# Turning shift rows and chunk results with transposing DMAs instead of TensorE, and spreading the last pair's shortcut over six turns

## The chip, the cores and the metric

The kernel runs on one core of a Trainium2 chip. The engines of the core work from instruction queues of their own and wait for each other through semaphores: TensorE (PE: matmuls, and PEld: the loading of their stationary operand), VectorE (DVE), ScalarE (ACT), GpSimd (POOL), and SyncE (SP), which here only issues DMAs. SBUF is the on-chip memory, PSUM holds what PE writes. The metric is the device time of one execution in microseconds, the median of several runs.

## The reference

Group normalisation of x, then eight heads of attention over the 2304 pixels of each image with 1x1 convolutions as projections, a shortcut convolution, and a residual:

```python
x: (4, 512, 48, 48) f32;  Wq, Wk, Wv, Wsc: (512, 512);  gamma: (1, 512, 1, 1)
xn = groupnorm(x, 32 groups)
q, k, v = Wq xn, Wk xn, Wv xn            # 8 heads of 64
attn = softmax(q^T k)                    # 2304 x 2304 for each image and head
out  = attn v                            # back to channels x pixels
result = x + gamma * out + Wsc xn
```

## The kernel before, in words

**Tiling.** The work is cut into 16 blocks (4 images x 4 pairs of heads, numbered g), and each block into 6 chunks of 384 query pixels (c = 0 to 5, `n` = 6g + c, 96 in all). A chunk runs over the 2304 keys in 18 steps of 128 keys, two steps to a **turn** (`m` = 0 to 8). Every f32 product is made of fp16 or bf16 parts, so that each of its matmuls has a partner for the lower half.

**One turn** issues on PE, in this order (from line 477): `top(U)` (scores for the row maxima of the chunk that comes 22 steps later), two `score` (L416 and L421: the scores of this chunk, the shift added by a matmul with the row CR in steps 0 and 1 of a chunk), `top(U + 1)`, two `weigh` (L439 to L442: the weighted sum of v for the two steps of the turn before, into the PSUM bank OB), and then half of a projection for the next block (`project`, 12 or 36 matmuls in sixths; L349 and L352). In turns 1 and 2 the projection is the shortcut of this chunk (`sc`); in turns 3 to 8 it is a part of k, q or v of the next block, in the order of `AHEAD`: chunks c = 0, 1, 2 make two k parts each (ready in turns 4 and 6), the others v and q. In the last pair (g = 15) turns 3 to 8 have no projection.

**The other engines.** ACT makes the exponentials (`exps`, L542) into PE32, of which four buffers exist, copies half of the maxima's scores to MXC, copies projections out of PSUM (`leave`), and evacuates OB into Oe in turn 0 of the next chunk (L556). DVE makes the maxima (L690, L693, L698), the lower halves of q and v, and the additions into xr: the shortcut (L672), and the attention's result (L680). POOL makes the lower half of each exponential (`split`, L895, two a turn), the differences of keys (`keys_diff`, L876, and `keys_diff_lower`, L882: for a k part two and three turns after it is ready, so in turns 6 and 7, and 8 and 0), and in some chunks the lower halves of the next image's normalised pieces (L970, turns 5 to 8 of chunks 3 to 5 in six of the blocks). A `weigh` waits for its `split`, a `split` for its exponential, and each queue is in order.

**The shift.** In turn 7 DVE reduces the maxima of the next chunk to c16, [128, 3, 128] fp16 with queries on the partitions (`shift_parts`, L703, L708, L710). In turn 8 PE turns it by three matmuls with an identity into free columns of the score banks (`shift_rows`, L368), ACT copies it to CR as fp16 (L535), and PE's first `score` of the next chunk waits for CR (line 406).

**The result of a chunk.** Oe has queries on the partitions and the sum of weights beside the sums. DVE inverts the sums in turn 1 of the next chunk (L717), POOL divides in turn 2 (L889; in the last pair ACT does, L565), PE turns the quotient, f32, in turn 0 of the chunk after that by three transposes into PJ (`turn`, L377), and DVE adds gamma times it into xr in turn 1 (L680), which SP then stores. SP's queue per chunk: the piece of x for the statistics or the normalisation, the store of chunk n-2, the load of chunk n+1's x into xr.

Of the kernel before, what the change touches and what calls it, by code (L numbers as in the profile page):

```python
# [35 lines left out]
CHUNKS = BLOCKS * NCH  # L36
DS = MT // 2
# [16 lines left out]
def slot_unit(n, m):  # L54

    if m == 0:
        return None
    if m < 3:
        return ("sc", n)
    g, c = divmod(n, NCH)  # L60
    if g + 1 == BLOCKS:
        return None
    kind, part = AHEAD[3 * c + (m - 3) // 2]
    return (kind, g + 1, part)


def done_at(M):

    if M < 0 or M % DS == 0 or M % DS % 2 == 1:
        return None  # L70
    return slot_unit(M // DS, M % DS)

# [9 lines left out]
def units():  # L82

    out = [(kind, 0, c) for kind, c in FIRST + BESIDE]
    for n in range(CHUNKS):
        if n >= 2:
            out.append(("f", n - 2))
        out += [done_at(n * DS + m) for m in range(DS) if done_at(n * DS + m)]
    out += [("f", CHUNKS - 2), ("f", CHUNKS - 1)]
# [13 lines left out]
LAST = (BLOCKS - 1) * NCH  # L103


def build(nc, x, wq, wk, wv, wsc, gamma, out):
    ctx = ExitStack()
    with ctx:
# [15 lines left out]
        attn = sb("attn", [P, 2, CH], F32)  # L124
# [3 lines left out]
        CR = sb("CR", [P, CH], F16)  # L128
# [43 lines left out]
        def shift_bank(n):  # L172
            if n == 0:
                return OB[:, 0:CH].rearrange("p (i n) -> p i n", i=QT)
            return SLS[:, 0:QT, CH:CH + P]

# [29 lines left out]
        s_wt = sem("s_wt")  # L206
        s_y = sem("s_y")
# [14 lines left out]
        s_cp = sem("s_cp")  # L222
# [35 lines left out]
        def _(sp):  # L258
# [14 lines left out]

            rows = x[0:C, :].rearrange("(t p) n -> p t n", p=P)
# [9 lines left out]
            for n in range(CHUNKS):  # L284
# [16 lines left out]
                if n + 1 < CHUNKS:  # L301
                    load_x(n + 1)
            store(CHUNKS - 2)
# [5 lines left out]
        def _(pe):  # L309
# [53 lines left out]
            def shift_rows(n):  # L363
                if n:
                    pe.wait_ge(s_exp, n * MT)
                pe.wait_ge(s_cc, 3 * n + 3)
                for i in range(QT):
                    last = pe.matmul(shift_bank(n)[:, i, :], c16[:, i, :], identh[:, :], start=True, stop=True)  # L368
                last.then_inc(s_cp, 1)

            def turn(n):
# [4 lines left out]
                for i in range(QT):  # L376
                    last = pe.transpose(PJ[:, i * P:(i + 1) * P], attn[:, n % 2, i * P:(i + 1) * P], identf[:, :])  # L377
# [19 lines left out]
            def score(n, k):  # L397
# [7 lines left out]
                if k == 0:  # L405
                    pe.wait_ge(s_cr, n + 1)
# [6 lines left out]
                if k < 2:  # L413
                    for h in range(2):
                        r = slice(h * D, (h + 1) * D)
                        pe.matmul(SL[k % 2][:, h, 0:CH], ones[r, :], CR[r, :], start=True, stop=False,  # L416
# [52 lines left out]
            for i, (kind, c) in enumerate(BESIDE):  # L469
                if i == len(BESIDE) - 1:  # L470
                    shift_rows(0)
# [5 lines left out]
            for n in range(CHUNKS):  # L477
                for m in range(DS):
# [18 lines left out]
                    if root_unit(n, m):  # L497
                        root(*root_unit(n, m)[1:])
                    if u and m % 2 == 0:
                        project(u, 4, 6)  # L500
            weigh(STEPS - 2)
            weigh(STEPS - 1)
            turn(CHUNKS - 2)
# [3 lines left out]
        def _(act):  # L507
# [25 lines left out]
            def shift_rows(n):  # L533
                act.wait_ge(s_cp, n + 1)
# [24 lines left out]
            def divide(n):  # L559

                act.wait_ge(s_rc, n + 1)
                act.wait_ge(s_pj, PLACE["f", n - 2] + 1)
                for h in range(2):
                    for i in range(QT):
                        one = act.activation(attn[:, n % 2, i * P + h * D:i * P + (h + 1) * D], Oe[:, h, i, 0:D],  # L565
                                             ACT.Copy, scale=rc[:, h, i, :])
# [433 lines left out]
```

## Time and profile before

| | us |
|---|---|
| median of 3 runs | 3211.22 (3210.1 to 3211.5) |
| the profiled execution | 3213.72 |
| its span, first to last instruction | 3212.0, at a mean granted TensorE clock of 0.999 |
| busy: PE / POOL / DVE / ACT | 3146.4 / 2811.2 / 2115.8 / 2095.1 |
| chain that ended last: PE / POOL / issue / ACT | 67% / 24% / 4% / 2% |
| DMA: mean rate, share of 16 engines (q1) | 26 GB/s, 7.4% |

Busy time is the time in which an engine worked on an instruction; matmuls overlap, so a busy PE is not one at its peak. The chain is followed back from the last instruction to what released each. A row of a timeline has the start in us, the duration in us, the engine, the line of the kernel, the operation and its tiles (out<-in), the count of instructions merged into it, and in brackets the idle time of the engine before it with what ended it. A row without a bracket began with no wait seen.

### The profile page before, as it was taken

Reading aid. Unit: us, or ns where it says so; the run is one execution under the profiler, and the core shown is the slowest. Engines: PE = TensorE matmul, PEld = TensorE weight load, DVE = VectorE, ACT = ScalarE, POOL = GpSimd, SP = SyncE. Lnnn points to the kernel's source line nnn. Section 1 sums busy time; section 2 is a strip of 40 time slices with the busy share of each in tenths; the row PEclk is TensorE's granted clock in tenths of the full one; section 3 lists DMA queues with packets and bytes.
Section 4 is the critical chain, followed back from the end, with each engine's and each line's share of the span. In section 5 each row is a group of like instructions: output and inputs, shape, how many; then the busy total and the mean of one; then the engine's idle time right before and its main releaser. Section 6 shows DMA issues by size and latency. Waiting matters only on the chain.

```text
span 3212.0 us, 119957 instructions
## 1 busy us (share of the span) xinstructions
PE 3146.4 (98%) x52880; PEld 2151.1 (67%) x52880; DVE 2115.8 (66%) x3539; ACT 2095.1 (65%) x3473; POOL 2811.2 (88%) x2128
## 2 busy tenths in 40 slices
PE   5999999999999999999999999999999999999998
PEld 3666676666667666676666766667666666766665
DVE  7767666666677666666667666666666666666674
ACT  3566676676666677676666567767666666666675
POOL 2688999999898899999989889999988989888898
PEclk9999999999999999999999999999999999999999
DMA  3010010100011001010001101001000000000000
GB/s 126 24 37 22 25 33 14 36 22 17 22 37 42 17 22 37 22 34 15 12 27 42 37 12 37 22 27 32 17 12 15 15 12 17 12 17 12 17 17 14
DMA packets 53030, 82.66 MB, mean 26 GB/s; under 512 B 4384, under 2 KB 50464, under 8 KB 52512
## 3 DMA queue, kind: packets, MB, share of 16 engines
q1 hardware_dynamic: 52512, 74.99, 7.4%
q8 instruction: 418, 6.85, 0.9%
q14 instruction: 100, 0.82, 0.1%
HBM read 56.10 MB, written 18.87 MB: 23 GB/s over the span
## 4 chain that ended last, share of the span: by engine, by line
PE 67%; POOL 24%; issue 4%; ACT 2%; DVE 0%; POOLq 0%; DVEq 0%
POOL PLO L895 19%; PE SL L421 17%; PE PJ L352 13%; PE OB L439 9%; PE MX L393 8%; PE OB L442 7%; PE OB L441 7%; PE PJ L349 4%; POOL DF L876 3%; POOL QK L882 2%; ACT PE L542 1%; PE PJ L377 1%; PE SL L416 1%; ACT QK L523 0%; PE SL L368 0%
## 5 line engine op out<-in xcount | busy, mean ns | idle before, releaser
L895 POOL TENSOR_TENSOR PLO<-PE 128x768 f16<-128x768 f32 x1728 | 2498.8, 1472 | 334.3 <-ACT PE L542 325.8
L542 ACT ACTIVATE PE<-SL 128x768 f32<-128x768 f32 x1728 | 1310.7, 815 | 14.7 <-PE SL L421 14.6
L439 PEld LDWEIGHTS OB<-V,PE 128*128 128x128 bf16 x10368 | 949.3, 99 | 278.7 <-POOL PLO L895 151.5
L690 DVE TENSOR_REDUCE mx<-MX 128x1 f32<-128x384 f32 x864 | 481.0, 557 | 969.6 <-PE MX L393 969.6
L439 PE MATMUL OB<-V,PE 128*128 128x65 f16 x10368 | 1069.6, 194 | 17.6 <-POOL PLO L895 16.8
L441 PE MATMUL OB<-V,PE 128*128 128x64 f16 x10368 | 1060.0, 193 | 0.0
L442 PE MATMUL OB<-V,PLO 128*128 128x65 f16 x10368 | 1059.0, 196 | 0.0
L550 ACT ACTIVATE MXC<-MX 128x384 f32<-128x384 f32 x864 | 424.6, 491 | 915.2 <-PE MX L393 901.6
L421 PE MATMUL SL<-QK 64*128 64x384 f16 x10368 | 999.4, 323 | 0.0
L441 PEld LDWEIGHTS OB<-V,PE 128*128 128x128 bf16 x10368 | 966.3, 97 | 0.0
L442 PEld LDWEIGHTS OB<-V,PLO 128*128 128x128 f16 x10368 | 965.8, 98 | 0.0
L693 DVE TENSOR_REDUCE mx<-MX 128x2 f32<-128x768 f32 x864 | 822.8, 952 | 29.9 <-PE MX L393 3.5
L421 PEld LDWEIGHTS SL<-QK 64*128 64x128 f16 x10368 | 505.5, 94 | 285.4 <-issue 0.8
L352 PE MATMUL PJ<-X,WT 128*128 128x384 f16 x3324 | 639.7, 326 | 0.0
L393 PE MATMUL MX<-QK 64*128 64x384 f16 x3456 | 572.4, 328 | 5.9 <-ACT MXC L550 2.9
L698 DVE TENSOR_REDUCE mx<-MXC 128x1 f32<-128x384 f32 x864 | 476.8, 552 | 4.2 <-ACT MXC L550 3.9
L352 PEld LDWEIGHTS PJ<-X,WT 128*128 128x128 f16 x3324 | 286.5, 98 | 136.3 <-issue 0.3
L393 PEld LDWEIGHTS MX<-QK 64*128 64x128 f16 x3456 | 182.0, 93 | 288.0 <-issue 180.7
L349 PE MATMUL PJ<-WT,X 128*128 128x128 f16 x3240 | 214.9, 219 | 0.0
L349 PEld LDWEIGHTS PJ<-WT,X 128*128 128x128 f16 x3240 | 186.0, 98 | 0.0
L882 POOL TENSOR_TENSOR QK<-DF,QK 128x384 f16<-128x384 f32 x96 | 89.2, 930 | 16.5 <-ACT QK L511 16.5
L535 ACT ACTIVATE CR<-SL 128x384 f16<-128x384 f32 x95 | 46.7, 491 | 84.5 <-PE SL L368 84.5
(108 smaller groups left out, 1435.8 us busy)
## 6 DMA issues: line engine op xcount, KB each, us to landing
gx<-x SPq DMA_DIRECT2D x36, 768.0 KB, 4.5
xr<-x SPq DMA_DIRECT2D x96, 192.0 KB, 2.4
out<-xr SPq DMA_DIRECT2D x96, 192.0 KB, 1.9
X<-x SPq DMA_DIRECT2D x6, 768.0 KB, 8.9
QK<-wk SPq DMA_DIRECT2D x1, 1024.0 KB, 12.7
QK<-wq SPq DMA_DIRECT2D x1, 1024.0 KB, 13.4
QK<-wv SPq DMA_DIRECT2D x1, 1024.0 KB, 14.1
QK<-wsc SPq DMA_DIRECT2D x1, 1024.0 KB, 15.3
```

What stands on the lines that cost most here:

```text
L349: last = pe.matmul(dst[:, i * P:(i + 1) * P], X[:, b % 2, p, t, m * P:(m + 1) * P], WT[:, 2, wp, t, j * P:(j + 1) * P], **edge)
L352: last = pe.matmul(dst[:, 0:CH], WT[:, WEIGHT[kind], wp, t, j * P:(j + 1) * P], X[:, b % 2, p, t, c * CH:(c + 1) * CH], **edge)
L393: last = pe.matmul(MX[:, h, 0:CH], QK[r, g % 2, QH, c * CH + i * P:c * CH + (i + 1) * P], QK[r, g % 2, KH, t * CH:(t + 1) * CH], start=Tru ...
L421: last = pe.matmul(SL[k % 2][:, h, 0:CH], QK[r, g % 2, a, keys], QK[r, g % 2, b, q], start=False, stop=a == DH and b == QL, skip_group_che ...
L439: pe.matmul(acc, upper, v[:, D:V1], start=k == 0 and h == 0 and i == 0, stop=False, skip_group_check=True)
L441: pe.matmul(acc[:, 0:D], upper, v[:, 0:D], start=False, stop=False, skip_group_check=True)
L442: last = pe.matmul(acc, PLO[:, s % PB, p0:p0 + P], v[:, D:V1], start=False, stop=k == MT - 1 and h == 1 and i == QT - 1, skip_group_check= ...
L542: act.activation(PE32[:, s % PB, :].rearrange("p (h n) -> p h n", h=2), SL[s % 2][:, :, 0:CH], ACT.Exp, scale=1.0 / SS).then_inc(s_exp, 1)
L690: nc.vector.tensor_reduce(mx3[:, n % 2, 0, k:k + 1], MX[:, 0, 0:CH], AX.X, ALU.max).then_inc(s_mxf, 1)
L693: nc.vector.tensor_reduce(mx3[:, n % 2, :, k], MX[:, :, 0:CH], AX.X, ALU.max).then_inc(s_mxf, 1)
L698: nc.vector.tensor_reduce(mx3[:, n % 2, 1, k:k + 1], MXC[:, :], AX.X, ALU.max).then_inc(s_mxr, 1)
L895: nc.gpsimd.tensor_tensor(PLO[:, s % PB, :], PE32[:, s % PB, :], PE32[:, s % PB, :].bitcast(BF16)[:, 1:4 * CH:2], ALU.subtract).then_inc(s ...
```

## The change

- The shift: PE's three matmuls, their columns in the score banks and ACT's copy go. SP issues one transposing DMA from c16 to CR, which becomes [128, 3, 128] of the same 384 columns. The first `score` waits for it. In SP's queue it stands after the load of chunk n+1's x; the one for chunk 0 right ahead of that for chunk 1.
- The result of a chunk: ACT divides, for all chunks, in turns 2 and 4 (three 64-column pieces of one head each), and writes an fp16 copy of the quotient in turn 6 (`result_upper`); POOL writes the rest as fp16 in turn 7 (`result_lower`), ahead of that turn's key difference and splits; SP turns both halves by one transposing DMA of 768 columns (`results`), behind the shift rows' DMA; DVE adds gamma times each into xr in turns 2 and 4 of the chunk after the one in which it is divided (`add_result`). `turn` on PE stays for the last chunk alone. attn has one buffer instead of two.
- The last pair: the shortcut is made one sixth a turn in turns 1 to 6, instead of half in each of turns 1 and 2.
- In the two chunks of an image where PE makes a small matmul for the next statistics in turn 8 (`root`), it still stands before the last third of the projection.

The core of the diff:

```diff
@@ planning
+    if n >= LAST:
+        return ("sc", n) if m < 7 else None
     if m < 3:
         return ("sc", n)
...
+def sixths(n, m):
+
+    if n >= LAST:
+        return m - 1, m
+    return (0, 3) if m % 2 else (3, 6)
@@ SyncE
+            def shift_rows(n):
+
+                sp.wait_ge(s_cc, 3 * n + 3)
+                sp.dma_start_transpose(CR[:, :, :], c16[:, :, :].rearrange("p i n -> p (i n)")).then_inc(s_cr, 16)
+
+            def results(n):
+
+                sp.wait_ge(s_al, n + 1)
+                sp.wait_ge(s_fo, n)
+                sp.dma_start_transpose(back[:, :, :], half[:, :, :].rearrange("p l n -> p (l n)")).then_inc(s_at, 16)
...
                 if n + 1 < CHUNKS:
                     load_x(n + 1)
+                if n == 0:
+                    shift_rows(0)
+                if n + 1 < CHUNKS:
+                    shift_rows(n + 1)
+                if n:
+                    results(n - 1)
@@ TensorE
-            def shift_rows(n):
-                if n:
-                    pe.wait_ge(s_exp, n * MT)
-                pe.wait_ge(s_cc, 3 * n + 3)
-                for i in range(QT):
-                    last = pe.matmul(shift_bank(n)[:, i, :], c16[:, i, :], identh[:, :], start=True, stop=True)
-                last.then_inc(s_cp, 1)
...
-                    pe.wait_ge(s_cr, n + 1)
+                    pe.wait_ge(s_cr, 16 * (n + 1))
...
-                    if m == 0 and n >= 2:
-                        turn(n - 2)
                     u = slot_unit(n, m)
-                    if u:
-                        project(u, *((0, 3) if m % 2 else (3, 4)))
-                    if m == DS - 1 and n + 1 < CHUNKS:
-                        shift_rows(n + 1)
@@ ScalarE
-                act.activation(CR[:, :].rearrange("p (i n) -> p i n", i=QT), shift_bank(n), ACT.Copy
-                               ).then_inc(s_cr, 1)
...
+            def divide(n, h):
+
+                if h == 0:
+                    act.wait_ge(s_rc, n + 1)
+                    act.wait_ge(s_al, n)
+                for i in range(QT):
+                    one = act.activation(attn[:, i * P + h * D:i * P + (h + 1) * D], Oe[:, h, i, 0:D],
+                                         ACT.Copy, scale=rc[:, h, i, :])
+                if h == 1:
+                    one.then_inc(s_wt, 1)
+
+            def result_upper(n):
+                act.wait_ge(s_wt, n + 1)
+                if n:
+                    act.wait_ge(s_at, 16 * n)
+                act.activation(half[:, 0, :], attn[:, :], ACT.Copy).then_inc(s_ah, 1)
...
-                    if m == 2 and n > LAST:
-                        divide(n - 1)
+                    if n and m in (2, 4):
+                        divide(n - 1, m // 2 - 1)
+                    if n and m == 6:
+                        result_upper(n - 1)
@@ VectorE
+            def add_result(n, l):
+
+                j = n // NCH % PAIRS
+                if l == 0:
+                    dve.wait_ge(s_pjd, LEFT["sc", n])
+                    dve.wait_ge(s_at, 16 * (n + 1))
+                else:
+                    dve.wait_ge(s_fh, n + 1)
+                nc.vector.scalar_tensor_tensor(
+                    out=xr[:, n % 3, :], in0=back[:, l * QT:(l + 1) * QT, :].rearrange("p i n -> p (i n)"),
+                    scalar=gam[:, j:j + 1], in1=xr[:, n % 3, :],
+                    op0=ALU.mult, op1=ALU.add).then_inc(s_fo if l else s_fh, 1)
...
-                    if m == 1 and n >= 2:
-                        leave(("f", n - 2))
...
+                    if m in (2, 4) and n >= 2:
+                        add_result(n - 2, m // 2 - 1)
@@ GpSimd
-                nc.gpsimd.tensor_tensor(
-                    attn[:, n % 2, :].rearrange("p (i h d) -> p h i d", h=2, d=D), Oe[:, :, :, 0:D],
-                    rc[:, :, :, :].to_broadcast([P, 2, QT, D]), ALU.mult).then_inc(s_wt, 1)
+            def result_lower(n):
+                pool.wait_ge(s_ah, n + 1)
+                nc.gpsimd.tensor_tensor(half[:, 1, :], attn[:, :], half[:, 0, :], ALU.subtract).then_inc(s_al, 1)
...
-                    if m == 2 and 0 < n <= LAST:
-                        divide(n - 1)
+                    if m == 7 and n:
+                        result_lower(n - 1)
```

## Rows read from the trace of the kernel before

**Rows 1.** Page, part 1: busy us, share of the span, instructions of each engine.

```profile
PE 3146.4 (98%) x52880; PEld 2151.1 (67%) x52880; DVE 2115.8 (66%) x3539; ACT 2095.1 (65%) x3473; POOL 2811.2 (88%) x2128
```

**Rows 2.** Timeline of ACT, evacuations into chunks 43 and 44: start us, us.

```profile
1505.58 0.50 ACT L556 ACTIVATE Oe<-OB 128x390 f32<-128x390 f32 x1 [0.40 <-PE OB L442]
...
1538.45 0.50 ACT L556 ACTIVATE Oe<-OB 128x390 f32<-128x390 f32 x1 [0.39 <-PE OB L442]
```

**Rows 3.** Timeline of PE, end of chunk 43 and start of 44.

```profile
1534.46 0.33 PE L368 MATMUL SL<-identh,c 128*128 128x128 f16 x3
1534.63 0.83 PE L349 MATMUL PJ<-WT,X 128*128 128x128 f16 x12
...
1535.57 0.33 PE L416 MATMUL SL<-CR,ones 64*128 64x384 f16 x2
...
1538.25 0.52 PE L377 MATMUL PJ<-identf,attn 128*128 128x128 f32 x3
1538.70 0.34 PE L393 MATMUL MX<-QK 64*128 64x384 f16 x2
...
1540.11 0.20 PE L439 MATMUL OB<-V,PE 128*128 128x65 f16 x1
...
1541.09 0.20 PE L439 MATMUL OB<-V,PE 128*128 128x65 f16 x1 [0.25 <-POOL PLO L895]
```

**Rows 4.** Timeline of POOL, turn 5 of chunk 43 to 0 of 44.

```profile
1523.06 2.89 POOL L895 TENSOR_TENSOR PLO<-PE 128x768 f16<-128x768 f32 x2 [1.36 <-ACT PE L542]
...
1537.25 0.93 POOL L882 TENSOR_TENSOR QK<-DF,QK 128x384 f16<-128x384 f32 x1
1538.12 4.33 POOL L895 TENSOR_TENSOR PLO<-PE 128x768 f16<-128x768 f32 x3
```

**Rows 5.** Timeline of DVE, turn 7 of chunk 43.

```profile
1530.66 1.45 DVE L710 SCALAR_TENSOR_TENSOR c<-cmx,c 128x6 f16<-128x6 f32 x1
```

**Rows 6.** Timeline, end of plain chunk 46 and start of 47.

```profile
1629.22 0.41 DVE L710 SCALAR_TENSOR_TENSOR c<-cmx,c 128x6 f16<-128x6 f32 x1
...
1633.63 0.33 PE L416 MATMUL SL<-CR,ones 64*128 64x384 f16 x2
...
1635.49 5.93 POOL L895 TENSOR_TENSOR PLO<-PE 128x768 f16<-128x768 f32 x4 [1.15 <-ACT PE L542]
...
1638.74 0.19 PE L439 MATMUL OB<-V,PE 128*128 128x65 f16 x1
```

**Rows 7.** Timeline of POOL, start of chunk 42, behind normalised pieces.

```profile
1472.12 5.92 POOL L895 TENSOR_TENSOR PLO<-PE 128x768 f16<-128x768 f32 x4 [0.45 <-ACT PE L542]
```

**Rows 8.** Groups of instructions by line: busy us, mean ns of one | idle before.

```profile
L882 POOL TENSOR_TENSOR QK<-DF,QK 128x384 f16<-128x384 f32 x96 | 89.2, 930 | 16.5 <-ACT QK L511 16.5
...
L680 DVE SCALAR_TENSOR_TENSOR xr<-PJ,gam,xr 128x384 f32<-128x384 f32 x96 | 58.4, 608 | 9.8 <-PE PJ L377 9.8
```

**Rows 9.** One line each, L710 and L267: duration ns min/median/max, first and last start us.

```profile
L710 DVE SCALAR_TENSOR_TENSOR c<-cmx,c x96: 186/778/1470, 91.3 to 3170.4; 128x6 f16<-128x6 f32 x96
...
L267 SPq DMA_DIRECT2D xr<-x x96: 327/328/1215, 20.2 to 3156.8; - x96
```

**Rows 10.** Page, part 6: DMA issues, KB each, median us from issue to landing.

```profile
gx<-x SPq DMA_DIRECT2D x36, 768.0 KB, 4.5
xr<-x SPq DMA_DIRECT2D x96, 192.0 KB, 2.4
out<-xr SPq DMA_DIRECT2D x96, 192.0 KB, 1.9
```

**Rows 11.** Timelines of POOL, PE and ACT, a chunk of the last pair.

```profile
3095.81 0.50 ACT L556 ACTIVATE Oe<-OB 128x390 f32<-128x390 f32 x1 [0.52 <-PE OB L442]
...
3123.78 0.50 ACT L556 ACTIVATE Oe<-OB 128x390 f32<-128x390 f32 x1 [0.52 <-PE OB L442]
...
3105.01 17.15 POOL L895 TENSOR_TENSOR PLO<-PE 128x768 f16<-128x768 f32 x12 [0.70 <-ACT PE L542]
...
3120.89 0.34 PE L416 MATMUL SL<-CR,ones 64*128 64x384 f16 x2 [0.36 <-issue]
```

More of the change, by code:

```diff
@@ L36 @@
 CHUNKS = BLOCKS * NCH
+LAST = (BLOCKS - 1) * NCH
 DS = MT // 2
@@ L60, in slot_unit @@
     g, c = divmod(n, NCH)
-    if g + 1 == BLOCKS:
-        return None
     kind, part = AHEAD[3 * c + (m - 3) // 2]
     return (kind, g + 1, part)
+def sixths(n, m):
+    if n >= LAST:
+        return m - 1, m
+    return (0, 3) if m % 2 else (3, 6)
 def done_at(M):
-    if M < 0 or M % DS == 0 or M % DS % 2 == 1:
+    if M < 0:
         return None
-    return slot_unit(M // DS, M % DS)
+    n, m = divmod(M, DS)
+    u = slot_unit(n, m)
+    return u if u and sixths(n, m)[1] == 6 else None
 def root_unit(n, m):
@@ L85, in units @@
     for n in range(CHUNKS):
-        if n >= 2:
-            out.append(("f", n - 2))
         out += [done_at(n * DS + m) for m in range(DS) if done_at(n * DS + m)]
-    out += [("f", CHUNKS - 2), ("f", CHUNKS - 1)]
+    out.append(("f", CHUNKS - 1))
     return out
@@ L123, in build @@
         xr = sb("xr", [P, 3, CH], F32)
-        attn = sb("attn", [P, 2, CH], F32)
+        attn = sb("attn", [P, CH], F32)
+        half = sb("half", [P, 2, CH], F16)
+        back = sb("back", [P, 2 * QT, P], F16)
         Oe = sb("Oe", [P, 2, QT, AW], F32)
@@ L206, in build @@
         s_wt = sem("s_wt")
+        s_ah = sem("s_ah")
+        s_al = sem("s_al")
+        s_at = sem("s_at")
+        s_fh = sem("s_fh")
         s_y = sem("s_y")
@@ L376, in turn @@
                 for i in range(QT):
-                    last = pe.transpose(PJ[:, i * P:(i + 1) * P], attn[:, n % 2, i * P:(i + 1) * P], identf[:, :])
+                    last = pe.transpose(PJ[:, i * P:(i + 1) * P], attn[:, i * P:(i + 1) * P], identf[:, :])
                 last.then_inc(s_pj, 1)
@@ L415, in score @@
                         r = slice(h * D, (h + 1) * D)
-                        pe.matmul(SL[k % 2][:, h, 0:CH], ones[r, :], CR[r, :], start=True, stop=False,
+                        pe.matmul(SL[k % 2][:, h, 0:CH], ones[r, :], CR[r, :, :], start=True, stop=False,
                                   skip_group_check=True)
@@ L489, in _ @@
                         weigh(s - 1)
-                    if m == 0 and n >= 2:
-                        turn(n - 2)
                     u = slot_unit(n, m)
-                    if u:
-                        project(u, *((0, 3) if m % 2 else (3, 4)))
-                    if m == DS - 1 and n + 1 < CHUNKS:
-                        shift_rows(n + 1)
-                    if root_unit(n, m):
+                    lo, hi = sixths(n, m)
+                    if u and root_unit(n, m):
+                        project(u, lo, hi - 2)
                         root(*root_unit(n, m)[1:])
-                    if u and m % 2 == 0:
-                        project(u, 4, 6)
+                        project(u, hi - 2, hi)
+                    elif u:
+                        project(u, lo, hi)
             weigh(STEPS - 2)
             weigh(STEPS - 1)
-            turn(CHUNKS - 2)
             turn(CHUNKS - 1)
@@ L557, in evacuate @@
                     "p (h i x) -> p h i x", h=2, x=OW)[:, :, :, 0:AW], ACT.Copy).then_inc(s_oe, 1)
[L559 to L566, printed above, removed]
-                one.then_inc(s_wt, 1)
+            def divide(n, h):
[12 more added lines that the diff above has]
+                act.activation(half[:, 0, :], attn[:, :], ACT.Copy).then_inc(s_ah, 1)
             def weights(w):
@@ L603, in _ @@
                     keys_diff_upper(("k", 0, i))
-            shift_rows(0)
             leave((BESIDE[-1][0], 0, BESIDE[-1][1]))
@@ L680, in leave @@
                     nc.vector.scalar_tensor_tensor(
-                        out=xr[:, n % 3, :], in0=src, scalar=gam[:, j:j + 1], in1=xr[:, n % 3, :],
+                        out=xr[:, n % 3, :], in0=src, scalar=gam[:, PAIRS - 1:PAIRS], in1=xr[:, n % 3, :],
                         op0=ALU.mult, op1=ALU.add).then_inc(s_fo, 1)
-                    dve.wait_ge(s_fo, n + 1)
-                    dve.sem_inc(s_pjd, 1)
+            def add_result(n, l):
[9 more added lines that the diff above has]
+                    op0=ALU.mult, op1=ALU.add).then_inc(s_fo if l else s_fh, 1)
             def top(U):
```

26 lines of the change are left out of this document (5 added, 21 removed).

## The prediction

> **What bounds the kernel now.** I read the page's busy shares first [rows 1]: PE is busy 98% of the span, POOL 88%, DVE and ACT two thirds. So PE is the bound on average, with POOL close behind. An average hides where in a chunk each of them is last, so next I read the timelines of PE and POOL across a chunk's end. One chunk takes 32.87 us, from one evacuation of the weighted sums to the next [rows 2], in nine turns of about 3.6 us.
>
> On PE [rows 3] the reader is to see three places. In turn 8 the three matmuls that turn the shift rows hold PE from 1534.46 to 1534.63, 0.17 us. In turn 0 the fp32 transposes hold it from 1538.25 to 1538.70, 0.45 us. In turn 1 the second `weigh` starts at 1541.09 behind a wait for POOL; the first one started at 1540.11, and its six steps of 0.093 us would have put the second at 1540.67, so PE loses 0.42 us there.
>
> On POOL [rows 4] the reader is to see where idle time (a bracket) stands. POOL waits 1.36 us for the exponentials of turn 5 and from 1523.06 on has no bracket until the last `split` of turn 0 ends at 1538.12 + 2 x 1.43 = 1540.98; PE starts 0.11 later. These 17.9 us are five pairs of splits (2.86 each), two lower halves of key differences (0.88 each, 1537.25 to 1538.12) and, with the remaining 1.9, the two differences themselves. So at this boundary POOL, not PE, is last. Key differences exist only in chunks whose number in the pair (c) is 0, 1 or 2, so this holds at the ends of those: 45 boundaries ahead of the last pair. After c = 3, 4, 5 POOL has rest: it waits 1.15 us before turn 0's splits in a plain chunk [rows 6], and 0.45 in the 18 chunks that also make normalised pieces [rows 7].
>
> **The change part by part.** *Off PE.* Each boundary loses 0.17 + 0.45 = 0.62 us of PE time [rows 3]; over 90 boundaries that would be 56 us, if PE were last at all of them.
>
> *POOL.* The division leaves turn 2, and the subtraction for the lower half comes into turn 7. It has the form of L882 (128x384, f32 minus f16 into f16): 930 ns busy [rows 8], 0.88 start to start [rows 4]. The place decides: turn 2 lies ahead of POOL's rest, turn 7 behind it. At the 45 boundaries after c = 0, 1, 2 the chain from turn 5's exponentials to turn 1's `weigh` has no rest to take it in, so it ends 0.88 later and none of PE's 0.62 is seen: PE waits longer. Freeing turn 2 returns nothing, since POOL waits ahead of turn 5's splits either way. That is 45 x 0.88 = +39.6.
>
> At the 27 plain boundaries after c = 3, 4, 5 the rest of 1.15 takes in the 0.88. POOL starts turn 0's splits at 1635.49 and ends the second at 1638.35, usable at 1638.46, and PE's second `weigh` starts at 1638.74 [rows 6]: a slack of 0.28. After the change turn 0 starts 0.17 earlier, the splits are usable at 1638.29, and PE is there at 1638.74 - 0.62 = 1638.12: it waits 0.17. Gain 0.45 each, 27 x 0.45 = -12.2. At the 18 with pieces the rest is 0.45 [rows 7]: the splits move 0.88 - 0.45 = 0.43 later, 0.28 of it is slack, and each is 0.15 slower: +2.7.
>
> *ACT.* It loses the CR copy and gets three 64-column divisions in each of turns 2 and 4 and a 384-column copy in turn 6. ACT is busy 65% [rows 1] and does these behind the exponentials of their turn, while it waits for PE: nothing. Without that cover, up to 0.3 us a turn.
>
> *DVE.* The last addition (turn 1, out of PSUM) becomes two, in turns 2 and 4, with both inputs in SBUF. L710 is such an instruction: six columns, 186 ns at least and 1470 at most [rows 9], which is the length of a split. So it waits for the POOL instruction under way, and I take it that POOL then waits for it. The Trainium skill ("SBUF — State Buffer", "Who interferes with whom") says that a two-input DVE instruction and a GpSimd instruction that reads SBUF hold a shared port in turn; the trace agrees. A 384-column one takes 0.61 by L680 [rows 8], with 1.43 of waiting 2.0 in the worst case; DVE is idle 34% of the span [rows 1], 1.2 us a turn. I cost it at nothing, since the wait is full only where a split has just begun, and at the upper end at 0.3 us in each of two turns, 180 x 0.3 = 54. POOL is held 0.4 us twice a chunk, ahead of its rest: nothing, except in the last pair.
>
> *SP and the transposing DMAs.* SP issues `shift_rows` once c16 is ready, behind `store` and `load_x`, which are done by turn 5, and ahead of `results`, which waits for POOL's lower half. Behind a late `shift_rows` only `results` is queued; for CR PE waits, with everything behind it. PE needs CR at turn 0's first score, 1535.57 [rows 3]; c16 was ready at 1530.66 + 1.45 = 1532.11 [rows 5]. That leaves 3.46 - 0.17 = 3.29 us; at a plain end 1633.63 - 1629.63 - 0.17 = 3.83 [rows 6]. No transposing DMA is in the trace. The nearest rows are a store of 192 KB at 1.9 us to landing and a load of 192 KB at 2.4; the far bound is the 768 KB piece at 4.5 [rows 10]. With the 0.33 that the issue takes [rows 9] these are 2.2, 2.7 and 4.8. An earlier landing than 2.2 gains nothing. CR is 96 KB, so I take 2.7: hidden. `results` has more than a turn and a half and is hidden at 4.8 too. The Trainium skill gives two answers: "Advanced Engine Details and Errata", "X-Bar Transpose (TRN2)", has such transfers as fast as regular ones, which agrees with my choice; by "VectorE: DVE Perf Modes", "The three transpose paths", one 128x128 block takes 1309 ns, an estimate of 4.2 for three in a row with the issue, and some 3255 us in all. No run here shows which.
>
> *The last pair.* A chunk takes 27.97 us [rows 11], with turns 1 and 2 long on PE, so that POOL waits there, and twelve splits on POOL without rest after them; it rests 2.1 in all. Spreading the shortcut removes the rests, and POOL's 25.9 + 0.88 + 2 x 0.4 (DVE) = 27.5 becomes the chunk. Four whole chunks gain 0.4, the last, without maxima, loses about 0.9: -1. The tail loses one turn and one DVE addition (0.45 and 0.61): -1.1. PE's wait for CR there, 0.36 now [rows 11], lies inside POOL's time.
>
> **The sum.** +39.6 - 12.2 + 2.7 - 1 - 1.1 = +28. The profiled execution took 3213.7 (span 3212.0 and 1.7 around it), so 3241.7; the median of the runs is 2.5 below it, so 3239.
>
> **The rivals.** *POOL isn't moved (faster).* Place: POOL in turns 5 to 8 after c = 0, 1, 2. If the lower half is taken in there, these boundaries stay as they are, since POOL is last at them already, and those with pieces gain 0.45 like the plain ones: -12.2 - 8.1 - 2.1 = -22, so 3189. The sum turns negative once POOL's chain ends less than 12/45 = 0.26 us later. For it: POOL's spans are rough in a profile, and short waits may hide in them. Against it: no bracket in 17.9 us. Only if POOL were last nowhere would all of PE's 56 us come, 3154. *The DMA lands late.* At 4.8 us it is 1.5 late after c = 0, 1, 2, where POOL's backlog hides it (turn 0's splits start at 1539.0 after the change; the exponentials would be there at about 1538.8), but 0.97 late at plain ends: 27 x 0.97 = 26, some 10 at the ones with pieces, some 8 in the last pair: +44, 3283. It begins to count from 3.8 us, and past 4.8 every microsecond costs about 95. The skill's 1309 ns would lie between. *It does not do what it says.* Spreading the shortcut may move nothing, as POOL sets the last pair: 2 us, inside the range.
>
> **How the numbers follow.** POOL last and the DMA hidden or nearly so: 0.55, 3239, own range 3220 to 3262 (the added 0.88 between 0.6 and 1.0, and some DVE delay). DMA late up to 4.8, or DVE's port waits nearly in full: 0.18, up to 3295. DMA later still: 0.10. POOL not moved: 0.14, 3189. All of PE's gain: 0.03. The range 3186 to 3295 holds the first, second and fourth; it leaves out the other two and a little of the edges. 0.2% of the time, 6.4 us, is about what a measurement can tell from no change: faster 0.15, within it 0.07 (the ways between 3189 and the forecast), slower 0.78.
>
> **What would show it.** In the profile after: POOL without a bracket from turn 5 to turn 1 after c = 0, 1, 2; PE's waits in turns 0 and 1 there grown from 0.42 to about 1.9 us together, chunks of 33.7 us there and 0.45 shorter than now at plain ends; L416 without idle time ahead of it; the transposes landing within 3.3 us of their release; DVE's additions of 0.5 to 2 us. The prediction is wrong if PE waits at L416 (DMA) or at L393 for DVE (ports), or if the chunks after c = 0, 1, 2 take 32.9 or less.

## The result and the profile after

The changed kernel takes 3242.8 us (median of 4 runs, 3241.8 to 3244.3) against 3211.4 for the kernel before in the same comparison: the ratio is 1.0098, with a 95% interval of 1.0086 to 1.011. The profiled execution took 3244.25, its span is 3242.4, and the granted clock was 0.998 (0.999 before). The forecast was 3239.

From the page of the kernel after: the busy shares; the chain that ended last, by engine; two groups (busy us, mean ns | idle before, releaser); and the two transposing DMAs (count, median us to landing).

```profile
PE 3112.3 (96%) x52307; PEld 2114.0 (65%) x52307; DVE 2245.6 (69%) x3634; ACT 2194.2 (68%) x4012; POOL 2882.4 (89%) x2133
...
PE 56%; POOL 33%; issue 4%; ACT 3%; DVE 1%; POOLq 0%; ACTq 0%; DVEq 0%
...
L913 POOL TENSOR_TENSOR PLO<-PE 128x768 f16<-128x768 f32 x1728 | 2552.5, 1502 | 293.9 <-ACT PE L547 290.2
...
L702 DVE SCALAR_TENSOR_TENSOR xr<-back,gam,xr 128x384 f32<-128x384 f16 x190 | 226.8, 1194 | 5.4 <-DMA back<-half 5.3
...
CR<-c SPq DMA_TRANSPOSE x96, 2.3
back<-half SPq DMA_TRANSPOSE x95, 2.8
```

PE's busy time is 34 us below [rows 1], and the kernel is 31 us slower: the work left PE, and its share of the last chain went to POOL, 33% where it was 24%. The waits say whom PE waits for (us, times, longest):

```profile
PEld OB L455 <- POOL PLO L913: 223.4, 569, 1.1
PE OB L455 <- POOL PLO L913: 72.1, 116, 1.0
ACT QK L521 <- POOL DF L898: 65.9, 46, 1.5
```

PE's matmuls of `weigh` waited 16.8 us for splits in the kernel before, and now 72.1. The third line is new in size (14.4 before): ACT's upper halves of key differences wait for the differences on POOL.

POOL's timeline at the end of a chunk with key differences, which answers to [rows 4]:

```profile
1539.09 2.89 POOL L913 TENSOR_TENSOR PLO<-PE 128x768 f16<-128x768 f32 x2 [1.05 <-ACT PE L547]
1541.94 1.00 POOL L898 TENSOR_TENSOR DF<-KF 128x384 f32<-128x384 f32 x1
1542.90 2.89 POOL L913 TENSOR_TENSOR PLO<-PE 128x768 f16<-128x768 f32 x2
1545.75 0.92 POOL L909 TENSOR_TENSOR half<-attn,half 128x384 f16<-128x384 f32 x1
1546.63 0.91 POOL L904 TENSOR_TENSOR QK<-DF,QK 128x384 f16<-128x384 f32 x1
1547.50 2.89 POOL L913 TENSOR_TENSOR PLO<-PE 128x768 f16<-128x768 f32 x2
1550.35 1.00 POOL L898 TENSOR_TENSOR DF<-KF 128x384 f32<-128x384 f32 x1
1551.31 2.89 POOL L913 TENSOR_TENSOR PLO<-PE 128x768 f16<-128x768 f32 x2
1554.16 0.92 POOL L904 TENSOR_TENSOR QK<-DF,QK 128x384 f16<-128x384 f32 x1
1555.04 5.74 POOL L913 TENSOR_TENSOR PLO<-PE 128x768 f16<-128x768 f32 x4
```

The reader is to see that no row after 1539.09 has a bracket, up to the end of turn 1's splits, and that L909 at 1545.75 stands in that row: 0.88 us from its start to the next one's. It is the lower half of the results, which the change put there. PE at the same place, which answers to [rows 3]:

```profile
1549.02 0.20 PE L455 MATMUL OB<-V,PE 128*128 128x65 f16 x1
...
1550.44 0.21 PE L455 MATMUL OB<-V,PE 128*128 128x65 f16 x1 [0.70 <-POOL PLO L913]
...
1552.29 0.33 PE L432 MATMUL SL<-CR,ones 64*128 64x384 f16 x2
...
1556.65 0.19 PE L455 MATMUL OB<-V,PE 128*128 128x65 f16 x1
...
1557.98 0.20 PE L455 MATMUL OB<-V,PE 128*128 128x65 f16 x1 [0.62 <-POOL PLO L913]
```

By the brackets PE waits for POOL 0.70 us in turn 8 and 0.62 in turn 1, where it waited 0.25 in turn 1 alone. Counted from start to start, as the prediction had its 0.42, these are 0.86 and 0.77: the first `weigh` starts at 1549.02 and at 1556.65, and 0.56 later the second was due. The score of turn 0, which needs the turned shift rows, starts without idle time. On DVE and SP's queue, when the shift rows were ready and when their DMA was issued:

```profile
1546.69 0.89 DVE L731 SCALAR_TENSOR_TENSOR c<-cmx,c 128x6 f16<-128x6 f32 x1
...
1547.61 1.19 SPq L284 DMA_TRANSPOSE CR<-c  x1
```

c16 is ready at 1547.58, the median of such DMAs lands 2.3 us after its issue, and PE wants the rows 4.7 us after c16. ACT's evacuations of the weighted sums, at the ends of this chunk and of a plain one, answer to [rows 2]:

```profile
1521.44 0.50 ACT L561 ACTIVATE Oe<-OB 128x390 f32<-128x390 f32 x1 [0.40 <-PE OB L458]
1555.17 0.50 ACT L561 ACTIVATE Oe<-OB 128x390 f32<-128x390 f32 x1 [0.40 <-PE OB L458]
...
1621.72 0.50 ACT L561 ACTIVATE Oe<-OB 128x390 f32<-128x390 f32 x1 [0.40 <-PE OB L458]
1653.65 0.50 ACT L561 ACTIVATE Oe<-OB 128x390 f32<-128x390 f32 x1 [0.40 <-PE OB L458]
```

33.73 us the one, 31.93 the other. All such distances of both traces, by the number c of the chunk in its pair, typical value in us; the last column sums the differences of the 89 chunks ahead of the last pair:

| c | before | after | sum |
|---|---|---|---|
| 0 | 32.45 | 32.86 | +5.7 |
| 1 | 32.88 | 33.75 | +13.0 |
| 2 | 32.86 | 33.73 | +12.3 |
| 3, plain / with pieces | 32.84 / 32.84 | 32.84 / 33.48 | +3.9 |
| 4, plain / with pieces | 32.37 / 32.38 | 31.92 / 32.57 | -3.0 |
| 5, plain / with pieces | 32.26 / 32.26 | 31.80 / 32.53 | -2.5 |

Together +29.5. The chunks c = 2 of blocks 1, 5 and 9, which have the square-root unit (`root`), are in the sums only: they take 34.84 for 34.19. With the start (-0.4), the last pair's first chunk (-0.7) and its other five (+2.2), and the tail (-0.2) that is the span's +30.4, but for rounding.

### The profile page after: what moved, and what is told of

The parts are those of the page before. It is cut to its first block, busy times and chain, and to the rows that moved or that the text cites. A ratio compares the mean times of both kernels' runs of the same rounds, so it can differ in the third digit from the quotient of the medians.

```text
span 3242.4 us, 119546 instructions
## 1 busy us (share of the span) xinstructions
PE 3112.3 (96%) x52307; PEld 2114.0 (65%) x52307; DVE 2245.6 (69%) x3634; ACT 2194.2 (68%) x4012; POOL 2882.4 (89%) x2133
## 4 chain that ended last, share of the span: by engine, by line
PE 56%; POOL 33%; issue 4%; ACT 3%; DVE 1%; POOLq 0%; ACTq 0%; DVEq 0%
POOL PLO L913 25%; PE SL L437 15%; PE PJ L376 12%; PE OB L455 8%; PE MX L409 7%; PE OB L458 6%; PE OB L457 6%; PE PJ L373 3%; POOL DF L898 3%; POOL QK L904 2%; ACT PE L547 2%; POOL half L909 2%; POOL X L988 1%; PE SL L432 1%; ACT QK L533 1%
## 5 line engine op out<-in xcount | busy, mean ns | idle before, releaser
L913 POOL TENSOR_TENSOR PLO<-PE 128x768 f16<-128x768 f32 x1728 | 2552.5, 1502 | 293.9 <-ACT PE L547 290.2
L455 PE MATMUL OB<-V,PE 128*128 128x65 f16 x10368 | 1074.8, 194 | 79.1 <-POOL PLO L913 72.1
L555 ACT ACTIVATE MXC<-MX 128x384 f32<-128x384 f32 x864 | 423.3, 490 | 874.8 <-PE MX L409 874.8
L702 DVE SCALAR_TENSOR_TENSOR xr<-back,gam,xr 128x384 f32<-128x384 f16 x190 | 226.8, 1194 | 5.4 <-DMA back<-half 5.3
L570 ACT ACTIVATE attn<-Oe,rc 128x64 f32<-128x64 f32 x570 | 155.6, 345 | 0.0
```

The source lines that it names most:

```text
L455: pe.matmul(acc, upper, v[:, D:V1], start=k == 0 and h == 0 and i == 0, stop=False, skip_group_check=True)
L913: nc.gpsimd.tensor_tensor(PLO[:, s % PB, :], PE32[:, s % PB, :], PE32[:, s % PB, :].bitcast(BF16)[:, 1:4 * CH:2], ALU.subtract).then_inc(s ...
```

## The experiments

My theory: POOL's extra 0.88 us in turn 7, where it is last, takes 0.88 at 45 ends, and PE's gain is seen only at the others. The rivals: DVE's additions hold POOL through the shared port; the DMA for the shift rows lands too late; the key differences hold the ends anyway, wherever the lower half stands. Chunk lengths below are distances of evacuations as in the table.

**The lower half two turns earlier.** `lower_turn5` (the comments behind # stand only here):

```
-                    if n and m == 6:     # ACT: result_upper
+                    if n and m == 4:
-                    if m == 7 and n:     # POOL: result_lower
+                    if m == 5 and n:
```

> The changed kernel with the fp16 copy on ScalarE in turn 4 and POOL's lower half in turn 5, ahead of the wait of 1.05 us that POOL has there, instead of in turn 7. Theory (place on POOL's chain): the 0.88 us come off the 45 boundaries after c = 0, 1, 2 (-39.6) and about 0.6 off the 18 with normalised pieces (-11), so about 3192 us, chunks of 32.9 us after c = 0, 1, 2. Rival (DVE's two-input additions hold up POOL, whose splits grew from 1472 to 1502 ns on average, 52 us of busy time in all, and that is the added time): nothing moves, 3240 to 3245 us.

It took 3209.0 us (10 runs, 3206.0 to 3212.7; ratio to before 0.9991, 0.9982 to 1.0). So one subtraction, with the copy on ACT that it waits for, moved by two turns and nothing removed, is worth 34 us: the place decides. POOL's split stays at 1502 ns on average with the same DVE additions, so the port isn't what made the change slow. But it missed 3192 by 17. The larger part is the 18 chunks with pieces, where I expected -11: undisturbed they take 33.46, 32.56 and 32.52, as in the kernel after. POOL's timeline in one of them shows why:

```profile
1226.08 3.20 POOL L913 TENSOR_TENSOR PLO<-PE 128x768 f16<-128x768 f32 x2 [0.73 <-ACT PE L547]
1229.25 0.91 POOL L909 TENSOR_TENSOR half<-attn,half 128x384 f16<-128x384 f32 x1
1230.12 0.92 POOL L988 TENSOR_TENSOR X<-gx,X 128x384 f16<-128x384 f32 x1
...
1242.17 8.64 POOL L913 TENSOR_TENSOR PLO<-PE 128x768 f16<-128x768 f32 x6
```

No row from 1226.08 to 1242.17 has a further bracket. With pieces POOL's last rest is the one ahead of turn 4's splits, so turn 5 (L909) is still behind it, and the subtraction stays on the chain; an earlier turn wasn't tried. The remaining shortfall lies at the other ends: chunks with c = 1 or 2 were 32.87 where undisturbed, yet many were 0.8 to 1.2 longer. The trace has the reason for these: the group of matmuls that needs the shift rows (busy us, mean ns | idle before), and one instance:

```profile
L432 PE MATMUL SL<-CR,ones 64*128 64x384 f16 x384 | 63.2, 323 | 15.6 <-issue 15.6
...
585.60 1.19 SPq L284 DMA_TRANSPOSE CR<-c  x1
...
589.64 0.34 PE L432 MATMUL SL<-CR,ones 64*128 64x384 f16 x2 [0.65 <-issue]
```

Without POOL's delay PE is back at this score 3.4 us after the issue (589.64 - 0.65 - 585.60), and this transfer landed after 3.9. Such landings are the tail that the prediction did not have; the DMA view of 585.4 to 588 shows what else moved:

```profile
q1 hardware_dynamic: 414, 0.10, 18.5%
q8 instruction: 1, 0.02, 2.2%
...
CR<-c SPq DMA_TRANSPOSE x1, 3.9
```

A packet of instruction fetch (q8) came in between; from its share in this view it took about 0.9 us of one of the 16 DMA engines (an estimate, 2.2% of 16 x 2.6 us). I read this view for each of the 95 later issues of three traces. All 49 landings above 3.5 us had such a packet between issue and landing (6 in the kernel after, 19 here, 24 in `three_moves` below), and 14 of the 224 landings up to 2.5 us. That ties them together; which delays which, and how, wasn't tried. Nor do the late ones fall by chance: `lower_turn5` and `both_moves` have their slow landings at the same 20 of the 95 issues (one is 3.53 us here), and five of the six of the kernel after are at the same issues in `halves_last`.

**The second key difference later.** Applied to the kernel before, `before_keys_later`, and with the move above to the one after, `both_moves`:

```
-                    done = done_at(n * DS + m - 2)
-                    if done and done[0] == "k":
-                        keys_diff_upper(done)
+                    for late in (2, 4):
+                        done = done_at(n * DS + m - late)
+                        if done and done[0] == "k" and late == 2 + 2 * (done[2] % 2):
+                            keys_diff_upper(done)
...
-                    for late, do in ((2, keys_diff), (3, keys_diff_lower)):
+                    for late, do in ((2, keys_diff), (3, keys_diff_lower), (4, keys_diff), (6, keys_diff_lower)):
...
-                        if done and done[0] == "k":
+                        if done and done[0] == "k" and (late >= 4) == (done[2] % 2 == 1):
```

> The kernel before with one thing moved: of each chunk's second key part (c = 0, 1, 2) the difference on POOL and its fp16 copy on ScalarE go from turn 8 to turn 1 of the next chunk, the lower half from turn 0 to turn 3. Theory: POOL's chain from turn 5 to turn 1 loses 0.96 + 0.88 us and PE is last there; the wait of 0.42 us at 45 boundaries goes, -19 us, about 3192 us. Rival (PE alone sets the time, the wait of 0.42 is hidden by later slack): 3211 us. Second rival (POOL becomes late in turns 2 and 3, where it also divides): 3200 to 3225 us.

3201.3 us (6 runs, 3199.6 to 3203.2; ratio 0.9968, 0.9957 to 0.998). Of the kernel before, PE's 0.42 at the ends was POOL's too: 24 of the 30 chunks with c = 1 or 2 and all 15 with c = 3 are 0.35 to 0.41 shorter, some -14.4 in all. The other six, in blocks 1, 5 and 9 with the square-root unit, are longer (33.44 for 32.87 at c = 1, 35.01 for 34.19 at c = 2), +4.2, which the expectation didn't have. That and 14.4 for 19 make most of the 9 us by which it missed 3192.

> The changed kernel with both moves: POOL's lower half in turn 5, and the second key part's POOL work in turns 1 and 3 of the next chunk. Theory: POOL is then nowhere last ahead of the last pair, and PE's 0.62 us at 90 boundaries and the 0.42 at 45 come through, less about 0.17 at each boundary where the splits of turn 0 are just late for PE: 3211 - 56 - 19 + 16 = 3152 us. Rival (port holds or the transposing DMAs take the gain): above 3200 us.

3193.5 us (4 runs, 3191.5 to 3194.3; ratio 0.9943, 0.9928 to 0.9958). Faster than before, and 41 short of what I expected. The idle time at L432 is again 34.1 us over 42 waits of matmuls and loads, some 17 for PE; the 18 chunks with pieces stay at 32.5 to 32.8 where 31.9 was wanted, some 12; the last five chunks are 2.6 longer than before; the rest I didn't take apart. With POOL freed, the DMA is the next that comes late.

**And the shift a turn earlier.** `three_moves` is `both_moves` with DVE's shift rows made in turn 6:

```
-                    if m == 7 and n + 1 < CHUNKS:    # shift_parts
+                    if m == 6 and n + 1 < CHUNKS:
```

> The changed kernel with POOL's lower half in turn 5, the second key part's POOL work in turns 1 and 3 of the next chunk, and the reduction to c16 at the end of DVE's turn 6 instead of 7, which is when its last maximum is there, so that CR's DMA has a turn more. With the first two alone PE waited for CR at about 20 boundaries, some 17 us in all, where the landing took 3.8 to 4.5 us instead of 2.3. Theory: this wait goes, and 3 us in the last pair: about 3173 us. Rival (the wait for CR isn't the landing of the DMA, or something else takes its place): 3190 us or more.

3181.9 us (4 runs, 3181.9 to 3183.9; ratio 0.9906, 0.9892 to 0.9921). It is faster than both kernels. SP's queue and PE at one end, and the source views of L432 (idle before it: us, times) and of L284:

```profile
1453.57 1.19 SPq L284 DMA_TRANSPOSE CR<-c  x1
...
1460.52 0.33 PE L432 MATMUL SL<-CR,ones 64*128 64x384 f16 x2
...
  issue: 0.2, 1
...
DMA to landing us min/median/max: 2.3/2.3/5.0
```

PE now wants the rows 6.9 us after the issue, and the same tail, up to 5.0 us and 27 of 95 above 2.5, costs 0.2 us in all. This shows that the waits of `both_moves` were these landings. Of the nine that were missed against the expectation 3.9 lie at c = 3, 4, 5 of the three blocks with statistics (0, 4 and 8), 0.43 a chunk longer; I put that down to DVE's fuller turn 6, which wasn't tried.

**The margin alone.** `shift_turn6` has only that last edit on the kernel after:

> The changed kernel with only the reduction to c16 at the end of DVE's turn 6 instead of 7, so that CR's DMA starts a turn earlier. Theory (POOL's backlog hides CR's late landings everywhere ahead of the last pair): only the last pair gets what PE waited for CR there, about 3 us: 3239 us. Rival (late landings are a part of the added time ahead of the last pair): 3225 us, since about 20 of them by some 0.8 us were seen once POOL's backlog was gone.

3241.8 us (4 runs, 3240.7 to 3242.0; ratio 1.0092, 1.0077 to 1.0107), not to be told from after. Ahead of the last pair it gains nothing, since POOL's backlog hides what lands late, and it loses 0.43 in nine chunks (+3.9). The last pair's five chunks are 4.2 shorter (136.11 for 140.33). So that is what late landings cost the kernel after.

**The lower half twice.** `lower_twice` adds POOL's subtraction once more behind the first, into a spare tile:

```
+                nc.gpsimd.tensor_tensor(spare[:, :], attn[:, :], half[:, 0, :], ALU.subtract)
```

> The changed kernel with the lower half's subtraction made twice in turn 7 (the first into a spare tile that nothing reads). Theory: another 0.88 us at the 45 boundaries after c = 0, 1, 2 and at the 18 with pieces, about 0.6 at the 27 plain ones, whose rest of 1.15 is mostly used up, and 0.88 in the five last: +76 us, about 3319 us. Rival (POOL has room, being busy 89%; ports or DMAs are the cause): under 3255 us.

3305.5 us (4 runs, 3304.1 to 3307.8; ratio 1.0295, 1.0278 to 1.0312). Chunks with c = 1 or 2 are 34.62, the second 0.87 exactly as the first, and so are those with pieces. The plain ones took only 0.15 more (31.95 for 31.80), where I had given them 0.6: most of it still fell into POOL's rest. That is 27 x 0.45 = 12 of the 14 us between the expectation and the time.

**The DMA later.** `one_more_turned` and `two_more_turned` issue one or two further transposing DMAs of c16, into spare tiles, ahead of the real one:

```
+                sp.dma_start_transpose(spare0[:, :, :], c16[:, :, :].rearrange("p i n -> p (i n)")).then_inc(s_sp0, 16)
```

> The changed kernel with one more transposing DMA of c16, into a spare tile that nothing reads, ahead of each one into CR in SP's queue. SP takes 1.19 us to issue one, so CR lands some 1.3 us later at all 95 boundaries, 3.6 us after c16 is ready. Theory (the DMA is hidden, with room left before turn 0's first score: 3.8 us at plain ends, 4.7 after c = 0, 1, 2, 2.4 in the last pair): only the last pair's five boundaries pay, +6, and a few whose landing is late already, +4: about 3253 us. Rival (the landing of CR is on the path): +1.3 x 95, 3360 us.

3267.1 us (4 runs, 3263.0 to 3269.1; ratio 1.0169, 1.0153 to 1.0184): +24, and 14 above what I expected. The undisturbed chunks keep their lengths (33.76, 31.80), so the median landing, now 3.6 us after c16, is still in time; what is longer are single chunks in which the landing was late, by 0.6 to 2 us, and the last five chunks (144.7).

> The same with two more transposing DMAs ahead of the one into CR: CR lands about 4.9 us after c16 is ready, which is the case of the prediction's late DMA at 4.8. Theory: hidden behind POOL's backlog after c = 0, 1, 2, 1.1 us late at 27 plain ends (+30), about 0.6 at 18 with pieces (+11), 2.4 in the last pair (+12), and +10 where it is late already: about 3306 us; by the prediction's own price of the late case +44 on 3243, 3287 us. Rival (each boundary pays the whole lateness): 3242 + 95 x 1.1 or more, over 3340 us.

3325.5 us (4 runs, 3322.3 to 3327.5; ratio 1.035, 1.0333 to 1.0367): +83, and 19 above what I expected. SP's queue and PE at a plain end:

```profile
1645.88 1.19 SPq L288 DMA_TRANSPOSE spare<-c  x1
1647.11 1.25 SPq L289 DMA_TRANSPOSE spare<-c  x1
1648.40 1.26 SPq L290 DMA_TRANSPOSE CR<-c  x1
...
1650.91 0.34 PE L440 MATMUL SL<-CR,ones 64*128 64x384 f16 x2 [1.05 <-issue]
```

Each issue holds SP's queue 1.2 us, the real one lands 4.9 us after c16 was ready, and PE waits 1.05. Plain chunks are 1.17 longer (32.97), 27 x 1.17 = 32 of the 83. The rest is mostly the tail, which now hits at any end. As rival, the late DMA had the right mechanism; its price for 4.8 us, +44 in all, was too low, since it took every landing to be the median.

**The additions with one input.** `one_input_adds`:

```
-                nc.vector.scalar_tensor_tensor(
-                    out=xr[:, n % 3, :], in0=back[:, l * QT:(l + 1) * QT, :].rearrange("p i n -> p (i n)"),
-                    scalar=gam[:, j:j + 1], in1=xr[:, n % 3, :],
-                    op0=ALU.mult, op1=ALU.add).then_inc(s_fo if l else s_fh, 1)
+                nc.vector.tensor_scalar(
+                    xr[:, n % 3, :], back[:, l * QT:(l + 1) * QT, :].rearrange("p i n -> p (i n)"),
+                    gam[:, j:j + 1], None, ALU.mult).then_inc(s_fo if l else s_fh, 1)
```

> The changed kernel with DVE's two additions of the turned halves replaced by two multiplications by gamma that read only the turned half from SBUF; the shortcut and x are left out of the output by this. Theory: DVE no longer waits for POOL (1.24 us become under 0.6) nor holds it (POOL's splits back from 1502 to about 1472 ns on average), but POOL took those holds out of its rest, so only the last pair gets faster, by 0.64 us a chunk: about 3240 us. Rival (port holds are the added time): 3190 to 3200 us.

3239.9 us (4 runs, 3238.6 to 3240.8; ratio 1.0085, 1.007 to 1.01), 2.8 below after, as much as the last five chunks lose (137.41 for 140.33). My 0.64 us for each of these isn't there: undisturbed ones are 0.23 shorter (26.94 for 27.17), and the largest part is one late landing that was less late (28.67 for 30.59). The groups of both instructions in this kernel:

```profile
L702 DVE TENSOR_SCALAR xr<-back,gam x190: 413/1045/2514, 173.1 to 3232.6; 128x384 f32<-128x384 f16 x190
...
L912 POOL TENSOR_TENSOR PLO<-PE 128x768 f16<-128x768 f32 x1728 | 2517.7, 1483 | 325.8 <-ACT PE L547 321.9
```

POOL's splits are 35 us less busy (1483 ns each for 1502), and next to nothing of it reaches the end of the program; only chunks with pieces are some 0.14 shorter (32.43 for 32.57 at c = 4). The test is weaker than meant: the multiplication, 413 ns at least, still took 1045 in the median, so it was held up too.

**Each part alone.** `shift_only` has the shift rows by DMA and the results as before, `results_only` the other way round:

> The kernel before with only the shift rows turned by the transposing DMA; results, division and the last pair's shortcut as before. Theory: PE's 0.17 us come through at the 45 ends of c = 3, 4, 5 (-7.6) and not where POOL is last; about 20 of 95 landings take 3.8 us or more, and a part of these is seen, since there is no added backlog on POOL to hide them (+5 to +8): 3208 to 3213 us, no change that can be measured. Rival (the DMA is hidden and PE is the bound everywhere): -0.17 x 95, 3196 us.

3206.8 us (10 runs, 3205.8 to 3209.0; ratio 0.9985, 0.9976 to 0.9994). It gains 0.17 at the ends where PE is last (c = 0, 4 and 5: 32.28, 32.20, 32.09) and 2.2 in the last five chunks; at c = 1 and 2 the ends stay at 32.87 or become longer by a late landing. I had expected no change that could be measured.

> The changed kernel with the shift rows turned by PE and copied by ScalarE as before. Theory: the cost lies in the results' part: +0.88 us at 45 ends, +0.15 at 18, -0.28 at 27 (PE's transposes of 0.45 gone, of which 0.17 turns into waiting), +2 in the last pair, -1 at the end: 3212 + 36 = 3248 us. Rival (the shift's DMA is the cost): about 3200 us.

3249.4 us (4 runs, 3249.0 to 3250.9; ratio 1.0118, 1.0101 to 1.0135). So the results, with POOL's lower half, make the loss (+37.9), and the shift rows take back 4.6; together +33.3, where the whole change measures +31.4.

**The shortcut in halves at the end.** `halves_last` puts the last pair's shortcut back to two turns, in `slot_unit` and `sixths`:

```
-    if n >= LAST:
-        return ("sc", n) if m < 7 else None
     if m < 3:
         return ("sc", n)
+    if n >= LAST:
+        return None
...
-    if n >= LAST:
-        return m - 1, m
```

> The changed kernel with the last pair's shortcut in halves in turns 1 and 2 as before. Theory: POOL waits in turns 1 and 2 again and still has the lower half in turn 7, so its chunks take 28.4 us instead of 27.2: 5 x 1.2 = +6, 3249 us. Rival (the spread does nothing): 3243 us.

3244.0 us (4 runs, 3243.4 to 3245.6; ratio 1.01, 1.0085 to 1.0115), not to be told from after, and 5 below what I expected. Its undisturbed chunks there take 28.1 where the change has 27.2, so the spreading does what it says. What makes up for it in the profiled executions is late landings: 4.2 us in the last pair of after, some 0.9 here.

## Why the prediction was right

**Off PE.** Forecast 0.62 an end. Where PE is last, that is what came off, less POOL's next wait: -0.45 forecast, -0.46 measured at c = 4 and 5. The rest that takes in POOL's 0.88 there isn't the one that the prediction named. The first row is of the kernel before, ahead of turn 7's splits in plain chunk 46, the second of the kernel after, turn 0's splits behind it:

```profile
1628.12 2.90 POOL L895 TENSOR_TENSOR PLO<-PE 128x768 f16<-128x768 f32 x2 [1.01 <-ACT PE L542]
...
1652.62 5.74 POOL L913 TENSOR_TENSOR PLO<-PE 128x768 f16<-128x768 f32 x4 [0.98 <-ACT PE L547]
```

The subtraction falls into the 1.01 ahead of turn 7's splits, and the 1.15 of turn 0 is nearly all still there. The prediction counted on the 1.15 alone; that is also why `lower_twice` cost so little at plain ends.

**POOL.** +0.88 at the ends after c = 0, 1, 2. At c = 1 and 2 the chunks are 0.87 longer, and take 33.75 and 33.73 for the 33.7 forecast. c = 0 and 3 are read together: the evacuation lies ahead of turn 1's second `weigh`, so a part of each delay falls into the next distance. Their +0.41 and 0.00 sum to +0.41; forecast was 0.88 - 0.45 = +0.43. With pieces a chunk is 0.64 to 0.73 above its plain neighbour, forecast 0.60, so these ends cost about 0.2 each and not 0.15. The sum ahead of the last pair: +30.1 forecast, +29.5 measured. For c = 0, 1 and 2 `lower_turn5` and `results_only` show that this is POOL's subtraction and its place; in the chunks with pieces both of its places lie behind POOL's last rest. PE's wait was forecast as 1.9 us: it is 0.86 and 0.77 by the same count, and 0.1 and 0.2 more ahead of the first `weigh` of each of these turns, 1.9 in all. Only the place was off, turn 8 instead of turn 0.

**The rival that POOL isn't moved** (3189) fell with the 33.73. That it is a matter of place and not of the change as such is shown by the same instructions two turns earlier, 3209.

**DVE.** The additions take 0.6 to 1.8 us, as the prediction wanted them, against POOL's splits:

```profile
L702 DVE SCALAR_TENSOR_TENSOR xr<-back,gam,xr x190: 607/1243/1806, 173.2 to 3234.5; 128x384 f32<-128x384 f16 x190
```

POOL's splits went from 1472 to 1502 ns, 52 us of busy time in all, and the longest addition is 1.2 us above the shortest, less than one split. I took this at nothing, and for the time of the kernel that holds to within 3 us by `one_input_adds`, as far as that test took the holds away (35 of the 52). PE doesn't wait for DVE's maxima more than it did: its loads ahead of `top` waited 27.8 us for them, and 32.4 before. The Trainium skill ("SBUF — State Buffer", "Who interferes with whom") has a DVE instruction with two inputs in SBUF contend with a GpSimd instruction that reads SBUF; the rows agree. The one-input multiplication was held up too, 1045 ns in the median for 413 at least. By the same section of the Trainium skill `tensor_scalar` can enter a two-port mode and then contends with GpSimd, which I overlooked when I chose that test; the rows agree with it.

**ACT** was costed at nothing. It is 99 us busier (2194 for 2095) and its share of the last chain is 3% for 2%; no run tried it by itself.

**The transposing DMA.** Taken at 2.7 us with the issue; it is 2.3, and 2.8 for the results. The landing times of [rows 10] count from the start of the issue, so the 0.33 that the prediction added for it was in them already:

```profile
L284 SPq DMA_TRANSPOSE CR<-c x96: 1179/1186/2152, 91.4 to 3201.8; - x96
...
DMA to landing us min/median/max: 2.3/2.3/4.5
```

Hidden ahead of the last pair, as forecast; after c = 0, 1, 2 POOL's backlog widens the 3.29 us to 4.7. A plain load of twice the bytes lands in 2.4 [rows 10]. The Trainium skill ("Advanced Engine Details and Errata", "X-Bar Transpose (TRN2)") has transposing DMAs as fast as regular ones, which agrees. From the 1309 ns a block of the Trainium skill ("VectorE: DVE Perf Modes", "The three transpose paths") three in a row would be 3.9, an estimate; these rows, 2.3 with the 1.19 of the issue, don't bear that out. What the prediction lacked is the tail, 12 of 95 above 2.5 us here.

**The last pair** is the term that was mis-sized: -1 forecast, +1.5 measured: -0.7 in its first chunk and +2.2 in the others. Undisturbed chunks are 27.2, 0.3 less than the forecast 27.5. The step that failed is "PE's wait for CR there, 0.36 now [...], lies inside POOL's time". PE and SP's queue at two of its ends:

```profile
3145.32 2.15 SPq L284 DMA_TRANSPOSE CR<-c  x1
...
3148.70 0.34 PE L432 MATMUL SL<-CR,ones 64*128 64x384 f16 x2 [0.97 <-issue]
...
3173.49 1.19 SPq L284 DMA_TRANSPOSE CR<-c  x1
...
3177.77 0.34 PE L432 MATMUL SL<-CR,ones 64*128 64x384 f16 x2 [1.87 <-issue]
```

Here PE comes to this score some 2.4 us after the issue, so the median landing just fits and a late one is seen in full: 0.97 and 1.87 us, in chunks of 28.2 and 30.6. `shift_turn6` takes the five from 140.3 to 136.1. The last chunk became 1.0 longer than before (27.48 for 26.44), where 0.9 was forecast. The tail gained 0.2 for 1.1: the turn of chunk 94 stood ahead of the last evacuation, so its 0.45 isn't in the tail, and behind it the last turn starts 0.5 sooner but takes 0.87 us for 0.55, which stays open.

The forecast is within 4 us of the median, and in part because errors cancel: +2.5 in the last pair and +0.9 in the tail, against -0.6 ahead of it and -0.4 at the start; the remaining 1 us is the step from the profiled execution to the median.

**PE's gain.** I gave 0.03 to 3154. Even with POOL out of the way in both places, 3193 was reached and 3182 with the DMA's margin too. The chunks that stay long there are those with pieces (32.5 to 32.8) and, at c = 1 and 2, those in blocks with the square-root unit (33.1 and 35.1). In the first POOL has no rest from turn 4 on, as shown above. In the second PE waits 1.3 us for ACT's copy of the maxima's scores (L555) once in each of the three blocks, 4.0 us in all in the kernel after and 2.9 before; no run took either away, so what they would give stays open.

## What to carry to other kernels

Taking work off the busiest engine pays only at the places where it is last, and what it is exchanged for is priced by where the next engine is last: the same 0.88 us instruction cost 34 us more two turns later, where POOL had no rest left to take it in. So place added work ahead of the idle wait of its engine, not behind. And give a DMA that stands between two engines the margin of its slow landings, not of its median: one turn more of it was worth 11.6 us once POOL was out of the way (`three_moves` against `both_moves`), and next to nothing while POOL was last (`shift_turn6`).

## What the hardware showed beyond that

A transposing DMA of 384 columns of fp16 (96 KB) lands in 2.3 us, of 768 columns in 2.8, and its issue holds SP's queue for 1.19 and 1.23 us, where a plain issue takes 0.33 [rows 9]. Its landings have a tail to 5.0 us, and all 49 above 3.5 us in three traces had an instruction fetch between issue and landing. A one-input DVE multiplication from fp16 into fp32, in SBUF, took 413 to 2514 ns beside POOL's splits.
